# Edge pass of a graph network on one NeuronCore: VectorE makes its cell one-hots chunk by chunk from a float16 number table in PSUM, instead of four chunks at once from an fp32 table

## The reference

```python
# layer 0, graph attention (feat = layernorm(x), 8 heads of 32)
ft = (feat @ W).reshape(n, 8, 32)
e = leaky_relu(a1[src] + a2[dst], 0.2)          # per edge and head
ex = exp(e - segment_max(e, dst)[dst])
out = segment_sum(ft[src] * (ex / segment_sum(ex, dst)[dst]), dst)
x = x + elu(out)
x = x + experts0(layernorm(x))                  # 6 experts, top 2
# layer 1, mean over the neighbours
agg = segment_sum(layernorm(x)[src], dst)
x = x + relu(layernorm(x) @ W_self + (agg / max(deg, 1)) @ W_neigh + b)
x = x + experts1(layernorm(x))                  # 16 experts, top 2
```

## Time and profile before

| | |
|---|---|
| time, median of 3 runs | 2217.66 us (2215.0 to 2220.96) |
| the profiled execution: its time, its span | 2218.17 us, 2216.4 us |
| PE busy | 1574.3 us (71%) |
| DVE busy | 1355.7 us (61%) |
| ACT busy | 1030.3 us (46%) |
| POOL busy | 1092.6 us (49%) |
| first and last indirect DMA of the edge pass issued at | 63.2 and 1106.1 us |

### The profile page before, as it was taken

How to read it: one execution, slowest core, us unless ns; L and a number is a source line. 1 busy time by engine, 2 the same in 40 slices (tenths; PEclk the granted TensorE clock), 3 DMA queues, 4 the chain that set the end, 5 groups by cost and what they waited for, 6 DMA issues and landing times. The chain is left out here.

```text
span 2216.4 us, 34830 instructions
## 1 busy us (share of the span) xinstructions
PE 1574.3 (71%) x8862; PEld 1023.6 (46%) x8901; DVE 1355.7 (61%) x2693; ACT 1030.3 (46%) x2370; POOL 1092.6 (49%) x1178
## 2 busy tenths in 40 slices
PE   6366666666666666666635299859999772999966
PEld 5122222222222222222214288737999762888855
DVE  7799999999999999999967211164100263211115
ACT  3667667767776776776614144233000021222323
POOL 1577777777777777777705523312111036122221
PEclk9698999999999999999965599969999875999988
DMA  7456666656666666666632377552999322666744
GB/s 227 117 159 169 167 167 169 175 162 169 174 166 168 170 174 164 168 176 163 167 97 78 109 222 233 167 199 76 271 278 280 99 63 100 209 216 212 219 145 129
DMA packets 275019, 375.25 MB, mean 169 GB/s; under 512 B 64697, under 2 KB 213491, under 8 KB 274792
## 3 DMA queue, kind: packets, MB, share of 16 engines
q1 hardware_dynamic: 211648, 203.72, 31.7%
q0 software_dynamic: 50208, 141.48, 23.7%
q10 hardware_dynamic: 13078, 29.08, 3.8%
HBM read 247.01 MB, written 127.55 MB: 169 GB/s over the span
## 5 line engine op out<-in xcount | busy, mean ns | idle before, releaser
L548 POOL DMA_INDIRECT f_buf<-ftab,scol x806 | 791.9, 982 | 279.0 <-issue 245.0
L886 DVE TENSOR_TENSOR f_cell_hot<-ps,hots 128x1800 bf16<-128x1800 f32 x155 | 313.7, 2027 | 3.3 <-issue 3.3
L662 PE MATMUL ps<-f_cell_hot,f_src_hot 128*128 128x450 bf16 x816 | 185.0, 359 | 141.6 <-DVE f_cell_hot L886 137.3
L771 ACT ACTIVATE f_rows_to<-iota,f_now_row 128x128 bf16<-128x128 f32 x816 | 249.2, 388 | 9.4 <-issue 9.3
L688 PE MATMUL ps<-f_buf,f_hot_e 128*32 128x272 f32 x1632 | 175.8, 512 | 83.7 <-DVE f_buf L935 82.2
L935 DVE TENSOR_TENSOR f_buf<-f_buf,ps 128x1024 f32<-128x1024 f32 x204 | 234.8, 1212 | 0.3 <-ACT ps L744 0.3
L662 PEld LDWEIGHTS ps<-f_cell_hot,f_src_hot 128*128 128x128 bf16 x816 | 72.5, 99 | 267.2 <-DVE f_cell_hot L886 108.2
L1761 POOL DMA_INDIRECT ys<-y_y,y_to x68 | 66.4, 977 | 202.1 <-DVE y_y L1850 191.7
L1094 PE MATMUL ps<-g_loaded,nb_parts 128*128 128x216 f16 x1500 | 139.6, 256 | 0.0
L1094 PEld LDWEIGHTS ps<-g_loaded,nb_parts 128*128 128x128 bf16 x1500 | 138.8, 98 | 0.0
L1072 DVE TENSOR_TENSOR accT<-accT,ps 128x36 f32 x124 | 23.9, 193 | 181.9 <-PE ps L1094 126.7
(11 more groups left out here) (436 smaller groups left out, 2973.4 us busy)
## 6 DMA issues: line engine op xcount, KB each, us to landing
y_wts<-in_L_ffn_w_dram SPq DMA_DIRECT2D x68, 512.0 KB, 4.0
xs<-zero_rows SPq DMA_DIRECT2D x33, 1032.0 KB, 21.2
counts<-f_stage SPq DMA_DIRECT2D x51, 450.0 KB, 3.5
x_wts<-in_L_ffn_expert_w_dram SPq DMA_DIRECT2D x84, 256.0 KB, 3.5
xs<-zero_rows SPq DMA_DIRECT2D x51, 403.1 KB
g_loaded<-counts ACTq DMA_DIRECT2D x10, 1350.0 KB, 13.7
f_buf<-ftab,scol POOLq DMA_INDIRECT x806
y_xr<-xs SPq DMA_DIRECT2D x34, 258.0 KB, 3.8
```

Of the source, the lines that this page charges most:

```text
L548: nc.gpsimd.indirect_dma_start(out=buf[u][:, j, :], out_offset=None, in_=s.ftab, in_offset=bass.IndirectOffsetOnAxis(ap=s.scol[:, b * CB + ...
L662: last = nc.tensor.matmul(cells[k % 2], src_hot[:, j, :], cell_hot[:, j, :], start=j % GC == 0, stop=j % GC == GC - 1)
L771: nc.scalar.activation(rows_to[:, j, :], s.iota[:], ACT.Abs, bias=now_row[b.side][:, half * n + j:half * n + j + 1])
L886: nc.vector.tensor_tensor(cell_hot[:, k * UC:(k + 1) * UC, :], bc(numbers, 1, UC), bc(now, 2, CELLS), ALU.is_equal).then_inc(last_ready if ...
```

## The change

`cell_hots` compared one table with four chunks' cell numbers in one instruction on 128 x 1800 elements, both operands spread by a stride of zero. Now it runs four instructions, one for each chunk, on 128 x 450 elements: the table is a float16 copy in PSUM, and the chunk's cell number comes in as a scalar of the partition (an fp32 column of `hots`). The result stays bf16 in SBUF, the semaphore is raised by the last of the four. The fp32 table shrinks to its first 128 numbers; the float16 table takes 225 words behind it in bank 7 and is copied once, as words, from ScalarE's `cell_numbers`. For this copy the wait on `cleared` (ScalarE's start-up copies) stands earlier.

```diff
-        numbers, cfirstw = ps[:, 7, 0:CELLS], ps[:, 7, CELLS:CELLS + NBT]
+        numbers, cfirstw = ps[:, 7, 0:W128], ps[:, 7, CELLS:CELLS + NBT]
+        half_numbers = ps[:, 7, W128:W128 + CELLS // 2].bitcast(F16)
...
             def cell_hots(b, k):
                 dve.wait_ge(built, b.quarter(k - UNITS))
                 at = b.i * CB + k * UC
-                now = s.hots[:, 0, at:at + UC] if isinstance(at, int) else s.hots[:, 0, bass.ds(at, UC)]
-                nc.vector.tensor_tensor(cell_hot[:, k * UC:(k + 1) * UC, :], bc(numbers, 1, UC), bc(now, 2, CELLS), ALU.is_equal).then_inc(last_ready if k == UNITS - 1 else hot_ready, 2 if k == UNITS - 2 else 1)
+                for j in range(UC):
+                    now = s.hots[:, 0, at + j:at + j + 1] if isinstance(at, int) else s.hots[:, 0, bass.ds(at + j, 1)]
+                    last = nc.vector.tensor_scalar(cell_hot[:, k * UC + j, :], half_numbers, now, None, ALU.is_equal)
+                last.then_inc(last_ready if k == UNITS - 1 else hot_ready, 2 if k == UNITS - 2 else 1)
...
-            nc.vector.tensor_copy(numbers, s.table[:])
+            nc.vector.tensor_copy(numbers, s.table[:, 0:W128])
+            dve.wait_ge(cleared, 1)
+            nc.vector.tensor_copy(half_numbers.bitcast(F32), cell_numbers[:].bitcast(F32))
```

## The result

The changed kernel takes 2242.13 us (2238.22 to 2243.45, 4 runs), the kernel before took 2218.86 us beside it (2215.00 to 2220.96, 4 runs). The ratio is 1.0107, with a 95% interval from 1.0094 to 1.0120: 23 us slower. The forecast of 2262 us had the sign and the mechanism; the loss was forecast at 44.5 us, about twice what it is. The profiled execution of the changed kernel took 2238.22 us, the lowest of its four.

What follows compares the result with a forecast made beforehand. VectorE was taken to set the 20.49 us batch period, GpSimd's floor being 20.0. 2218.2 + 47.5 (issues held longer) - 3 (start) = 2262.7 us profiled, 2262 us forecast; range 2200 to 2290 us.

Steps and rivals of the forecast that it cites:

- The unit: VectorE's four new instructions: 0.36 us each, 1.45 us together, 0.50 us less than before; bounds 0.25 and 0.60 us each.
- rival 2: Two-byte elements from PSUM go one by one: unit 2.38 us, VectorE stays the pace, 2284 us; chance 0.18.
- The pace passes to GpSimd: VectorE's step falls to 19.0 us, under GpSimd's floor; the period becomes 20.0 us plus what its issues are held.
- The mask's 1.00 us: Mask (L879) behind `own_tops` (L900): it begins 9.72 us after L900's end; the eighth issue is held, 1.00 us lost per batch.
- The 0.5 us of `own_tops`: L900 behind the gather: it holds an issue for 0 to 1.1 us per batch; the middle, 0.5, was taken.
- The sum: Held 1.00 + 0.5 instead of 0.49 us per batch, 1.01 more; 47 periods, +47.5 us, less 3 us: 2262 us.
- The 3 us for the start: Eight units made ahead of the loop save 4 us, of which 3 were counted.
- the prediction's random positions: Argument against rival 1: at a random position `own_tops` and the mask cost 0.5 us each, 1.0 together, per batch.
- The address instruction in front of each new one costs nothing: On VectorE, address instructions ahead of the new ones add no time, the engine being busy 0.36 us meanwhile.
- Rival 1: GpSimd sets the pace and is held little: period falls towards 20.0 us, 2192 us at the floor; chance 0.20.
- rival 3: No change to be measured: the two instructions hold about 0.5 us together as today, 2216 us; chance 0.12.
- the signs named for a right forecast: Starts 0.36 us apart, free issues 1.25, mean issue above 1.03; L735 and L898 idle about a us in most steps.

Runs made afterwards that it cites:

- run 10: Changed kernel, but the new instructions read ScalarE's float16 table in SBUF instead of the one in PSUM: 2244.92 us.
- run 9: Kernel before, its fp32 table in PSUM, but the unit made chunk by chunk, without the two-byte table: 2321.38 us.
- run 1: Changed kernel, with `mx` and `own_window` put in PSUM, so neither `own_tops` nor the mask has two operands in SBUF: 2193.25 us.
- run 2: Changed kernel, with a batch's twelve cell numbers copied to a fixed place, so the new instructions need no address instructions: 2257.99 us.
- run 7: Changed kernel, with `mx` and `own_window` in PSUM and the twelve cell numbers copied to a fixed place: 2194.81 us.
- run 4: Kernel with all units made by one instruction as before, on the float16 table, and `mx` and `own_window` in PSUM: 2215.43 us.
- run 3: Changed kernel, but the third unit, between `own_tops` and the mask, made by one instruction again, on the float16 table: 2216.52 us.
- run 8: Changed kernel plus a useless VectorE copy of 225 words between the third unit and `batch_tops`: 2219.10 us.
- run 5: Changed kernel, with `own_window` alone in PSUM: 2216.46 us.
- run 6: Changed kernel, with `mx` alone in PSUM: 2215.92 us.

## Why the prediction was right, and where its size came from

**The unit.** Right: two elements at a time, 0.36 us an instruction, 1.44 us a unit. Both bounds exist as well, 0.25 us with the table in SBUF (run 10) and 0.60 us with the fp32 table (run 9); the scalar in fp32 did not stand in the way, and so the condition of rival 2 was false and its price right. The 120 cycles of the Trainium skill ("VectorE: DVE Perf Modes", section "The TRN2 errata") gave 1.44 us for the new unit as well, and 2.00 for the old one, which pays 1.95: here the two can hardly be told apart.

**"The pace passes to GpSimd."** Right (runs 1 and 10): in the changed kernel VectorE's time no longer counts by itself.

**The mask's 1.00 us** (the term "L879 behind L900"). The mechanism was right in its detail: 10.95 us between the two, and where `own_tops` has held an issue, the eighth after it begins 0.16 to 0.18 us into the mask and is held 0.97 or 0.98 us, forecast 0.15 and 1.00. The size per batch was not: 0.70 us, the mean of 40 batches. In ten of them, one in each lap, the distance is 11.27 to 11.30 us, longer by about the 0.35 us with which the prediction let an issue slip by, and 0.07 us is held; where `own_tops` has held nothing and an issue began with it, the mask holds about 0.82. The cause is the wait at L917, which came with the longer loop. In run 2, without it, the term is 0.95 us.

**The 0.5 us of `own_tops`.** Too large: 0.26 us per batch (0.34 in run 2). I took the middle of an open range; in 12 of 40 batches an issue begins together with `own_tops` or just ahead of it, and is not held, a case that the earlier trace rows showed at 810.75.

**The sum.** Forecast 1.01 us more per batch, measured 0.54 by the table. Of the 0.47 us between them, 0.30 are the mask's and 0.24 are `own_tops`'; other held issues add under 0.1 us. 0.54 x 47 = 25 us; the first gather came 2.0 us earlier in the profiled execution (61.16 us), together 23 us, the difference of the medians. The two profiled executions themselves differ by 20.1 us (2238.22 and 2218.17), and their last gathers by 21.1 (1127.21 and 1106.14), so the sum is good to some 3 us. The 3 us for the start can't be ascribed to the units made there: run 7 also makes them chunk by chunk, and its first gather is at 63.19 us, while run 4 has the old unit and its first gather at 61.28. The case that the forecast had in mind, no wait at the laps, is run 2: 1.28 us held and 2258 us, where 1.5 and 2262 were forecast. So 16 of the 20 us between forecast and result go with a wait that the prediction did not know of (run 2 also has one small copy per step more). And 1.02 us held is also what the prediction's random positions would cost, 1.0; it takes runs 3 and 8, which shift one distance, to tell the two apart.

**"The address instruction in front of each new one costs nothing."** True inside a step, and false for the loop: 9 more comparisons and 9 more address instructions in each of four steps are 72 more instructions in the body, and with them VectorE stands still 3.3 us a lap. The page of before could not show this, since it had no such wait. It did not lengthen the changed kernel (GpSimd sets its pace, and its 0.33 us at L917 even helped, run 2), but it takes 0.7 to 0.8 us per batch of VectorE's time where VectorE sets the pace (run 9), and is why VectorE trails in run 1 and not in run 7.

**The rivals.** Rival 1's 2192 us is what the change is worth once nothing is held (run 1, 2193 us); rival 3 is where chance shifts of the distance end (runs 3 and 8). Of the signs named for a right forecast, the starts 0.36 us apart and the free issues 1.25 us apart came. The mean issue was to rise from 977 ns to over 1030 and rose to 1011, short of it. ScalarE waits for gathers 1.4 us per batch on average, in 29 of 48 steps, and L901 for TensorE 0.96 us, in only 20 of them, where most steps were named.

## What to carry to other kernels

Before shortening the busiest engine's work, compute the floor of every other engine that never waits for a semaphore: GpSimd showed 7 tenths busy here and was 2.4% from setting the pace. Where two engines disturb each other, what a shorter instruction does is decided by the distances between the disturbing instructions, so add up their positions, and remove the disturbance (one operand in PSUM) in the same edit: the change alone lost 23 us, the moved operands alone won 0.1%, both together won 25 us. An edit that splits one instruction into four with an address each also makes a loop body longer, and here that had a price of its own at the jump back.

## What the runs showed of the hardware that was not expected

- **With its loop body grown, VectorE stood still at the start of each lap.** It stood about 2.8 to 4.0 us in the changed kernel (72 instructions more) and in runs 1, 5, 6, 8, 9 and 10, and not in runs 2, 3 (48 more), 4 and 7; the instruction packets between 100 and 1100 us were 62 to 66 with the wait and 11 or 12 without. That the length decides fits all of them, but no run varied the length alone. The Trainium skill, "Runtime: NRT & Kernel Launch", section "Instruction fetch mechanics", says that a taken branch to a target outside a window of two pages has to fetch the page first; the packets agree with that, but no run shows the window or to which engine the packets belong.
- **TensorE's clock fell and the time did not follow it.** Mean granted clock between 100 and 1100 us (the third number from the end; 0.94 before the change) in the changed kernel, run 1 and run 4:

```profile
100.00:1100.00 1000.00, 718.69 (x3124) 264.47 (x3124) 835.01 (x1708) 698.31 (x1614) 768.32 (x761) 0.84 0.60 164
```
```profile
100.00:1100.00 1000.00, 724.76 (x3248) 270.36 (x3248) 864.67 (x1769) 714.14 (x1652) 740.94 (x783) 0.86 0.63 170
```
```profile
100.00:1100.00 1000.00, 655.54 (x3193) 232.54 (x3194) 926.26 (x1311) 713.80 (x1652) 742.62 (x784) 0.95 0.62 169
```

  0.84, 0.86 and 0.95 of full speed, though run 1 is the fastest of the three and run 4 is 27 us faster than the changed kernel: the clock did not decide between them. It is part of the chain behind a late gather: L645 took 969 ns on average in the changed kernel, 650 before. From 814 to 824 us the granted clock was 0.50 (the lower level, 1.2 GHz), after 4 us in which TensorE was busy for 2.1, and the four of L645 at 818.62 us took 3.78 us; those of the earlier trace rows took 1.88 us at a granted clock of 1.00.
